# A decoder layer on one core: the first stage runs its pairs of sequences further ahead of the attentions

## The chip, the core and the metric

The kernel runs on one core of a Trainium2 chip. The metric is the device time of one execution in microseconds (us), lower is better. The core's engines work side by side and meet only through semaphores: TensorE (PE, matmuls and transposes), VectorE (DVE), ScalarE (ACT), GpSimd (POOL) and SyncE (SP, which only starts DMAs here).

## The reference, cut to what matters

The input is 16 sequences of 128 tokens with 128 features. There are three stages, each with a residual and a layer norm behind it. The first ("mixer") and the second (attentions and feed-forward) look like this; the third, a small per-position network, isn't touched by the change.

```python
# first stage, per sequence
x = u @ W_in + b_in                       # 128 -> 3*128
uc = dw_causal_conv(x.T, short_w, short_b)   # 3 taps per channel
q, k, v = uc[:, :D], uc[:, D:2*D], uc[:, 2*D:]
v = dw_causal_conv(k * v, inner_w, inner_b)  # 4 taps
y = (q * v).T @ W_out + b_out
x1 = layernorm(u + y)
# second stage: 16 heads of 64, self attention, then cross attention
a = attention(x1, x1, mask, sa_wq, sa_wk, sa_wv, sa_wo, sa_bo)
x = layernorm(x1 + a, ln1_g, ln1_b)
a = attention(x, ctx, mask, ca_wq, ...); x = layernorm(x + a, ...)
x = layernorm(x + fc2(gelu(fc1(x))), ...)
```

## The kernel before, in words

There is no scheduler. Each engine has a list of steps written out by hand in `mixer_and_attentions`, the same loop over a period number `p` on every engine, and each engine works through its own list in order. A step's semaphore waits hold up whatever is behind it on that engine.

**Items.** There are 32 attention items: item n is the self attention of sequence n for n < 16, then the cross attention of n - 16. Period `p` has, on PE: `x_transpose(p-4)`, the two value products `v_half(p)`, four `unit`s (query and key products of the next pair of items, alternating in banks 0 and 1), the four transposes of the probabilities of item p-1, `out_proj(p-2)`, `scores(p+1)` and `p_v(p-1)`. DVE takes row maxima (`maxima`, four groups of four heads, the first two at the end of the period before), reciprocals, copies keys (`k_out`) and transposed probabilities (`pt_out`) out of PSUM, and does `residual(p-2)` with its statistics. ACT does the exponentials (`exps`, four groups), and copies queries, values and outputs (`q_out`, `v_out`, `ot_out`). POOL multiplies the probabilities by the reciprocals (`normalise(p, g)`) and does the power for the standard deviation, gains and shifts.

**The first stage** handles pairs m = 0..7 of sequences inside the same loop, one step of a pair every second period. `pair_of(p, lead)` gives pair m in period p = 2m - lead, and nothing otherwise. With the leads before (PROJECT 6, CONVOLVE 4, TRANSPOSE 3), pair m goes like this:
- p = 2m-6 (even): projections of channels 0 and 1 on PE (`projection`), `projected` on ACT, two earlier taps for each on DVE (`earlier_taps`);
- p = 2m-5 (odd): the same for channel 2, then on POOL `keys_values` (edge fix and the product k*v) and `output_bias`;
- p = 2m-4 (even): `inner_convolution` (DVE, four taps), `gate` (POOL), `mixer_output` (PE), `mixer_residual` and `mixer_statistics` (DVE), `mixer_deviation` (POOL), `mixer_shift` (DVE), `mixer_normal` (ACT, at the end of its list);
- p = 2m-3 (odd): `x1_transposes` (PE), `x1_high` (ACT) and `x1_low` (DVE), which split the result in two parts for the attention's products, and `mixer_residuals` (POOL).
The attention's products of pair m start in period 2m-2 and wait for `x1_low(m)` (semaphore x1lo).

**Period 0 is not the first.** The loop starts at FIRST = -7; units start in period -2. The tail of odd periods also splits raw input and weights into a high part (ACT: `x_high`, `weight_high`) and a low part (DVE: `x_low`, `weight_low`). Banks: 4 and 5 hold projections and the p_v products, 6 the values, 7 (W_BANK) everything 128 wide, and before the change `mixer_output` too; `x1_transposes` went to bank 5.

## Time and profile before

| what | value |
|---|---|
| median of 3 runs | 558.27 us (556.9 to 560.64) |
| the profiled execution's own time | 560.64 us |
| its span in the trace | 558.8 us |
| PE busy | 475.0 us, 85% of the span |
| DVE busy | 412.6 us, 74% |
| ACT busy | 370.5 us, 66% |
| POOL busy | 262.8 us, 47% |

The span is the time from the first to the last instruction; the metric adds 1.84 us around it. A period is best measured between the starts of two `scores` groups on PE: scores(0) starts at 42.75 us, scores(1) at 56.40, scores(2) at 70.10, scores(12) at 235.52. From there to the last one at 460.92 us a period takes 11.92 us. The names of tiles in the trace have their bank and pair numbers left out: `late_bank` is any PSUM bank, `R`, `N`, `C`, `G`, `KV` and `yT` are tiles of the first stage, `at_...` tiles of the attention.

### The profile page before, as it was taken

Reading aid. Unit: us, or ns where it says so; the run is one execution under the profiler, and the core shown is the slowest. Engines: PE = TensorE matmul, PEld = TensorE weight load, DVE = VectorE, ACT = ScalarE, POOL = GpSimd, SP = SyncE. Lnnn points to the kernel's source line nnn. Section 1 sums busy time; section 2 is a strip of 40 time slices with the busy share of each in tenths; the row PEclk is TensorE's granted clock in tenths of the full one; section 3 lists DMA queues with packets and bytes.
Section 4 is the critical chain, followed back from the end, with each engine's and each line's share of the span. In section 5 each row is a group of like instructions: output and inputs, shape, how many; then the busy total and the mean of one; then the engine's idle time right before and its main releaser. Section 6 shows DMA issues by size and latency. Waiting matters only on the chain. (4 is left out here: it accounts for less than half of the span.)

```text
span 558.8 us, 13934 instructions
## 1 busy us (share of the span) xinstructions
PE 475.0 (85%) x4518; PEld 433.8 (78%) x4518; DVE 412.6 (74%) x1925; ACT 370.5 (66%) x1390; POOL 262.8 (47%) x348
## 2 busy tenths in 40 slices
PE   1477778888788887899999999999999999989573
PEld 1376667777677877899999999999999987779462
DVE  3666787887869777787777887777887776468774
ACT  3335776938667484788888688887688886534534
POOL 0423364544645455454554445554545545333561
PEclk9988899999979998999999999999999999997765
DMA  7910000000000000060000000000000000050003
GB/s 220 272 64 2 1 2 2 2 1 2 0 2 2 2 1 2 2 110 4 3 2 2 1 4 1 2 1 2 3 2 2 1 4 0 1 156 2 3 18 75
DMA packets 14663, 13.64 MB, mean 24 GB/s; under 512 B 2816, under 2 KB 12288, under 8 KB 14464
## 3 DMA queue, kind: packets, MB, share of 16 engines
q1 hardware_dynamic: 14448, 12.49, 8.3%
q8 instruction: 37, 0.61, 0.5%
q14 instruction: 34, 0.28, 0.2%
q10 hardware_dynamic: 144, 0.26, 0.2%
HBM read 11.57 MB, written 1.18 MB: 23 GB/s over the span
## 5 line engine op out<-in xcount | busy, mean ns | idle before, releaser
L580 ACT ACTIVATE P<-P,at_negmax 128x128 f32<-128x128 f32 x512 | 198.9, 396 | 55.6 <-DVE at_negmax L723 55.6
L952 POOL TENSOR_TENSOR P<-P,at_inv 128x512 f32<-128x512 f32 x128 | 131.9, 1042 | 151.4 <-DVE at_inv L733 151.4
L749 DVE COPY at_PT<-late_bank 128x512 f32<-128x512 f32 x128 | 87.7, 687 | 33.3 <-PE late_bank L442 33.1
L723 DVE CUSTOM_DVE_ANT_0 P<-late_bank,maskb 128x128 f32<-128x128 f32 x512 | 111.6, 286 | 0.5 <-PE late_bank L459 0.5
L580 ACT ACTIVATION_READ_ACCUMULATOR P<-P,at_negmax 128x1 f32 x512 | 100.0, 195 | 0.0
L442 PE MATMUL late_bank<-ident,P 128*128 128x128 f32 x512 | 78.9, 279 | 15.2 <-DVE at_negmax L723 13.3
L442 PEld LDWEIGHTS late_bank<-ident,P 128*128 128x128 f32 x512 | 60.9, 143 | 23.1 <-issue 18.9
L459 PE MATMUL late_bank<-at_k,at_q 64*128 64x128 f32 x1024 | 65.8, 278 | 1.0 <-DVE at_k L741 1.0
L459 PEld LDWEIGHTS late_bank<-at_k,at_q 64*128 64x128 f32 x1024 | 59.7, 188 | 5.3 <-issue 1.8
L474 PE MATMUL late_bank<-at_PT,V 128*64 128x128 f32 x1024 | 63.0, 276 | 0.0
L474 PEld LDWEIGHTS late_bank<-at_PT,V 128*64 128x64 f32 x1024 | 55.2, 137 | 3.9
L590 ACT ACTIVATE at_q<-late_bank 128x512 f32<-128x512 f32 x64 | 37.8, 591 | 27.5 <-PE late_bank L75 27.5
L741 DVE COPY at_k<-late_bank 128x512 f32<-128x512 f32 x64 | 44.1, 689 | 13.4 <-PE late_bank L75 12.6
L723 DVE DVE_READ_ACCUMULATOR2_ANT at_negmax<- 128x1 f32 x512 | 42.5, 83 | 0.0
L970 POOL TENSOR_TENSOR at_N<-at_N,row_ln_g 128x128 f32<-128x128 f32 x32 | 15.2, 474 | 57.4 <-DVE at_N L774 57.4
L599 ACT ACTIVATE V<-late_bank 128x512 f32<-128x512 f32 x64 | 37.7, 589 | 0.0
L733 DVE RECIPROCAL at_inv<-at_total 128x4 f32<-128x4 f32 x128 | 21.2, 170 | 19.0 <-ACT P L580 18.9
L607 ACT ACTIVATE at_OT<-late_bank 128x512 f32<-128x512 f32 x64 | 34.2, 591 | 0.0
L490 PE MATMUL late_bank<-wo_sa,at_OT 128*128 128x128 f32 x256 | 31.2, 275 | 0.0
L490 PE MATMUL late_bank<-wo_ca,at_OT 128*128 128x128 f32 x256 | 31.2, 275 | 0.0
L648 ACT ACTIVATE N<-R,shift,rstd 128x128 f32<-128x128 f32 x16 | 7.0, 487 | 36.0 <-DVE shift L871 36.0
L1381 POOL TENSOR_TENSOR ffrstd<-ffmv,half_neg 128x4 f32<-128x4 f32 x16 | 16.3, 1019 | 30.9 <-DVE ffmv L1274 30.9
(179 smaller groups left out, 1109.2 us busy)
## 6 DMA issues: line engine op xcount, KB each, us to landing
ctxT_raw<-in_ctxT SPq DMA_DIRECT2D x1, 1024.0 KB, 8.9
out<-xres SPq DMA_DIRECT2D x4, 224.0 KB, 2.5
x<-in_xT SPq DMA_DIRECT2D x1, 768.0 KB, 7.5
xres<-in_x SPq DMA_DIRECT2D x1, 768.0 KB, 12.3
...
```

Source lines behind the costliest of these rows:

```text
L442: last = nc.tensor.transpose(banks[T_BANK[g % 2]][:, h * 128:(h + 1) * 128], P[:, n % 2, HQ * g + h, :], k.ident[:])
L459: last = nc.tensor.matmul(score_bank(h), q[rows, t % 2, h // 2, pair], kk[rows, t % 2, h // 2, pair], start=True, stop=True)
L474: last = nc.tensor.matmul(banks[O_BANK[h // 8]][part:part + 64, h // 2 % 4 * 128:(h // 2 % 4 + 1) * 128], V[:, n % 2, h * DH:(h + 1) * DH] ...
L490: last = nc.tensor.matmul(banks[W_BANK][:, 0:128], OT[:, n % 2, c, :], out_w[att(n)][:, c, :], start=(c == 0), stop=(c == H // 2 - 1))
L580: last = nc.scalar.activation(P[:, n % 2, h, :], P[:, n % 2, h, :], ACT.Exp, scale=-1.0, bias=negmax[:, n % 2, h:h + 1], accum_out=total[: ...
L590: nc.scalar.activation(q[:, t % 2, u:u + 2, :], banks[UNIT_BANK[0]][:].rearrange("p (h l) -> p h l", h=2), ACT.Copy, scale=NEG_SCALE).then ...
L599: nc.scalar.activation(V[:, n % 2, half * 512:(half + 1) * 512], banks[V_BANK][:], ACT.Copy).then_inc(v_ok, 1)
L607: nc.scalar.activation(OT[:, n % 2, 4 * o:4 * o + 4, :], banks[O_BANK[o]][:].rearrange("p (c l) -> p c l", c=4), ACT.Copy).then_inc(ot_ok, 1)
L723: last = nc.vector.tensor_tensor_reduce(P[:, n % 2, h, :], score_bank(h), k.maskb[:, cols(n)], scale=1.0, scalar=3.0e38, op0=ALU.add, op1= ...
L741: nc.vector.tensor_copy(kk[:, t % 2, u - 1:u + 1, :], banks[UNIT_BANK[1]][:].rearrange("p (h l) -> p h l", h=2)).then_inc(k_ok, 1)
L749: nc.vector.tensor_copy(PT[:, HQ * g:HQ * g + HQ, :], banks[T_BANK[g % 2]][:].rearrange("p (h l) -> p h l", h=HQ)).then_inc(pt_ok, 1)
L952: nc.gpsimd.tensor_tensor(tile, tile, inv[:, n % 2, HQ * g:HQ * g + HQ].unsqueeze(2).to_broadcast([128, HQ, 128]), ALU.mult).then_inc(norm ...
```

## The change

The leads of the first stage are now PROJECT 8, CONVOLVE 6, OUTPUT 5, TRANSPOSE 4 with FIRST = -9. A pair m goes: channels 0 and 1 at p = 2m-8 (even), channel 2 and k*v at 2m-7 (odd), convolution and gate at 2m-6 (even), output product, residual and statistics at 2m-5 (odd), normalisation, transposes and both splits at 2m-4 (even), `mixer_residuals` at 2m-3 (odd). `mixer_output` writes to bank 5 and `x1_transposes` to bank 7. Steps stand at other places in the lists.

```diff
-        FIRST, FIRST_UNITS = -7, -2
+        FIRST, FIRST_UNITS = -9, -2
-        PROJECT, CONVOLVE, TRANSPOSE = 6, 4, 3
+        PROJECT, CONVOLVE, OUTPUT, TRANSPOSE = 8, 6, 5, 4
-        C_BANK, X1T_BANK = (4, 5, 4), 5
+        C_BANK, OUT1_BANK, X1T_BANK = (4, 5, 4), 5, W_BANK
@@ p_v(n)
-                    wait(pe, x1lo, ...)
+                if pair_of(n + 1, OUTPUT) is not None:
+                    wait(pe, r1_ok, pair_of(n + 1, OUTPUT) + 1)
@@ out_proj(n)
-                if pair_of(n + 2, CONVOLVE) is not None:
-                    wait(pe, r1_ok, pair_of(n + 2, CONVOLVE) + 1)
+                if pair_of(n + 2, TRANSPOSE) is not None:
+                    wait(pe, x1lo, pair_of(n + 2, TRANSPOSE) + 1)
@@ PE's list
                 transposes(p - 1, 1)
-                if p >= 0:
-                    mixer_output(p, pair_of(p, CONVOLVE))
                 unit(p, 2)
+                x1_transposes(p, pair_of(p, TRANSPOSE))
                 transposes(p - 1, 2)
...
                 projection(p, pair_of(p, PROJECT), 1)
-                if p < 0:
-                    mixer_output(p, pair_of(p, CONVOLVE))
-                x1_transposes(p, pair_of(p, TRANSPOSE))
+                mixer_output(p, pair_of(p, OUTPUT))
                 out_proj(p - 2)
@@ ACT's list
                 q_out(p, 0)
-                exps(p, 2)
+                mixer_normal(pair_of(p, TRANSPOSE))
                 ot_out(p - 2, 0)
                 ot_out(p - 2, 1)
+                exps(p, 2)
+                x1_high(pair_of(p, TRANSPOSE))
                 q_out(p, 2)
                 v_out(p, 1)
                 projected(pair_of(p, PROJECT), 0)
                 projected(pair_of(p, PROJECT), 1)
                 projected(pair_of(p, PROJECT - 1), 2)
-                x1_high(pair_of(p, TRANSPOSE))
                 exps(p, 3)
-                mixer_normal(pair_of(p, CONVOLVE))
@@ DVE's list
                 pt_out(p - 1, 1)
-                reciprocals(p, 2)
-                mixer_residual(pair_of(p, CONVOLVE))
                 pt_out(p - 1, 2)
                 k_out(p, 3)
                 pt_out(p - 1, 3)
-                mixer_statistics(pair_of(p, CONVOLVE))
                 earlier_taps(pair_of(p, PROJECT), (0, 1))
                 earlier_taps(pair_of(p, PROJECT - 1), (2,))
                 x1_low(pair_of(p, TRANSPOSE))
+                mixer_residual(pair_of(p, OUTPUT))
+                mixer_statistics(pair_of(p, OUTPUT))
+                reciprocals(p, 2)
+                if p % 2 and p >= -5:
+                    x_low((p + PROJECT + 1) // 2)
+                if p in (-5, -4, -3):
+                    weight_low(SA[p + 5])
...
+                elif p in (2, 4, 6):
+                    weight_low(CA[p // 2 - 1])
+                elif p in (8, 10):
+                    context_low((p - 8) // 2)
                 residual(p - 2)
                 reciprocals(p, 3)
                 maxima(p + 1, 0)
                 maxima(p + 1, 1)
-                mixer_shift(pair_of(p, CONVOLVE))
+                mixer_shift(pair_of(p, OUTPUT))
-                if p % 2 and p >= -3:
-                    x_low((p + PROJECT + 1) // 2)
-                elif p in (1, 3, 5):
-                    weight_low(CA[p // 2])
@@ POOL's list
-                normalise(p, 0)
                 gate(pair_of(p, CONVOLVE))
-                for g in range(1, QUARTERS):
+                for g in range(QUARTERS):
                     normalise(p, g)
+                mixer_deviation(pair_of(p, OUTPUT))
                 inverse_deviation(p - 2)
-                mixer_deviation(pair_of(p, CONVOLVE))
-                mixer_residuals(pair_of(p, TRANSPOSE))
                 keys_values(pair_of(p, PROJECT - 1))
                 output_bias(pair_of(p, PROJECT - 1))
+                mixer_residuals(pair_of(p, TRANSPOSE - 1))
```

PE at the end of an even period, here p = 6, before; `w3` are the first stage's input weights, `wo_sa` the attention's output weights, L490 is `out_proj`, L459 is `scores`:

```order
L73 MATMUL late_bank5<-xT_hi,w3_hi 128x256 [waits mx_x1lo,mx_tap_ok,at_ot_ok]
L74 MATMUL late_bank5<-xT_lo,w3_hi 128x256
L75 MATMUL late_bank5<-xT_hi,w3_lo 128x256
L490 MATMUL late_bank7<-wo_sa,at_OT 128x128 [waits at_r_ok,mx_r1_ok,at_xT_lo,at_ot_ok]
L490 MATMUL late_bank7<-wo_sa,at_OT 128x128 x7
```

And in the changed kernel, where L491 is `out_proj`:

```order
L73 MATMUL late_bank5<-xT_hi,w3_hi 128x256 [waits mx_r1_ok,mx_tap_ok,at_ot_ok]
L74 MATMUL late_bank5<-xT_lo,w3_hi 128x256
L75 MATMUL late_bank5<-xT_hi,w3_lo 128x256
L491 MATMUL late_bank7<-wo_sa,at_OT 128x128 [waits at_r_ok,mx_x1lo,at_xT_lo,at_ot_ok]
L491 MATMUL late_bank7<-wo_sa,at_OT 128x128 x7
```

Nothing stands between the last projection and `out_proj` in either; `out_proj`'s wait on r1_ok (DVE's `mixer_residual`) became a wait on x1lo (DVE's `x1_low`).

DVE behind the last copies of an even period, p = 4, in the changed kernel (L743 `pt_out`, L822 `earlier_taps`, L872 `x1_low`, L877 `weight_low`, L755 `residual`):

```order
L735 COPY at_k<-late_bank1 128x512 [waits at_s_mm,at_u_mm]
L743 COPY at_PT<-late_bank3 128x512 [waits at_pv_mm,at_t_mm]
L822 SCALAR_TENSOR_TENSOR C<-late_bank4,taps,C 128x2x127 [waits mx_c_ok]
L822 SCALAR_TENSOR_TENSOR C<-late_bank5,taps,C 128x2x127 [waits mx_c_ok]
L822 SCALAR_TENSOR_TENSOR C<-late_bank4,taps,C 128x2x126 [waits mx_tap_part]
L822 SCALAR_TENSOR_TENSOR C<-late_bank5,taps,C 128x2x126 [waits mx_tap_part]
L872 TENSOR_TENSOR x1T_lo<-late_bank7,x1T_hi 128x256 [waits mx_x1hi]
L727 RECIPROCAL at_inv<-at_total 128x4 [waits at_exp_ok]
L877 TENSOR_TENSOR ca_wk_lo<-ca_wk_raw,ca_wk_hi 128x1024 [waits mx_w_hi]
L755 TENSOR_TENSOR at_R<-late_bank7,xres 128x128 [waits mx_res1_ok,at_n_ok,at_o_mm]
```

`x1_low` now stands in the same period as the four taps of channels 0 and 1, and behind them; `weight_low` stands ahead of `residual`, where before it stood between two pairs of maxima groups.

ACT in the middle of an even period, p = 4, in the changed kernel (L588 `q_out`, L646 `mixer_normal`, L605 `ot_out`, L578 `exps`, L654 `x1_high`, L597 `v_out`, L636 `projected`):

```order
L588 ACTIVATE at_q<-late_bank0 128x512 [waits at_s_mm,at_u_mm]
L646 ACTIVATE N1<-R1,shift1,rstd1 128x128 [waits mx_res1_ok,mx_xT1_mm,mx_shift1_ok]
L646 ACTIVATE N1<-R1,shift1,rstd1 128x128
L605 ACTIVATE at_OT<-late_bank4 128x512 [waits at_o_mm,at_pv_mm]
L605 ACTIVATE at_OT<-late_bank5 128x512 [waits at_o_mm,at_pv_mm]
L578 ACTIVATE P,at_total<-P,at_negmax 128x128 [waits at_max_ok]
L578 ACTIVATE P,at_total<-P,at_negmax 128x128 x3
L654 ACTIVATE x1T_hi<-late_bank7 128x256 [waits mx_xT1_mm]
L597 ACTIVATE V<-late_bank6 128x512 [waits at_pv_mm,at_v_mm]
L636 ACTIVATE C<-late_bank4,conv_bias,taps 128x256 [waits mx_y_ok,mx_c_mm]
L636 ACTIVATE C<-late_bank5,conv_bias,taps 128x256 [waits mx_y_ok,mx_c_mm]
```

`mixer_normal` moved from the end of the list, where it stood behind `exps(p, 3)` in the period of its statistics, to the period after them.

## Rows read from the trace of the kernel before

**Rows 1.** Windows: stretch and length, busy us by engine, PE clock, DMA, GB/s.

```profile
70.10:102.74 32.64, 26.56 (x267) 24.09 (x267) 25.89 (x113) 23.71 (x92) 15.55 (x19) 1.00 0.01 2
102.74:135.84 33.10, 26.71 (x271) 24.23 (x270) 26.68 (x117) 22.65 (x87) 17.68 (x23) 1.00 0.01 1
135.84:171.07 35.23, 29.30 (x270) 26.83 (x270) 26.42 (x117) 22.88 (x87) 17.65 (x23) 0.90 0.01 2
171.07:204.14 33.07, 26.68 (x271) 24.21 (x270) 26.68 (x117) 22.65 (x87) 17.65 (x23) 1.00 0.01 1
204.14:235.52 31.38, 26.96 (x262) 24.72 (x261) 24.31 (x110) 20.86 (x83) 17.48 (x23) 0.95 0.01 2
119.69:135.84 16.15, 13.21 (x134) 11.87 (x133) 11.57 (x56) 11.12 (x45) 6.65 (x9) 1.00 0.01 2
135.84:152.79 16.95, 13.51 (x139) 12.37 (x138) 14.85 (x63) 11.54 (x44) 11.02 (x14) 1.00 0.01 1
259.32:271.23 11.91, 11.91 (x128) 11.18 (x128) 9.40 (x48) 9.32 (x39) 5.98 (x8) 1.00 0.01 1
```

**Rows 2.** Waits from 70.1 to 221.5 us: who for whom, us, times, longest.

```profile
PE late_bank L442 <- DVE at_negmax L723: 12.2, 9, 2.0
PE late_bank L523 <- POOL yT L998: 8.5, 5, 2.1
```

**Rows 3.** Timeline of PE in two periods: start, us, what, idle before.

```profile
126.34 0.63 PE L442 MATMUL late_bank<-ident,P 128*128 128x128 f32 x4 [1.04 <-DVE at_negmax L723]
...
129.15 0.50 PE L73 MATMUL late_bank<-sa_wv_hi,x1T_hi 128*128 128x512 f32 x1 [1.47 <-ACT V L599]
...
133.96 1.95 PE L490 MATMUL late_bank<-wo_sa,at_OT 128*128 128x128 f32 x16
...
143.17 0.63 PE L442 MATMUL late_bank<-ident,P 128*128 128x128 f32 x4 [1.72 <-DVE at_negmax L723]
...
147.36 0.71 PE L523 MATMUL late_bank<-w_out,yT 128*128 128x128 f32 x4 [1.73 <-POOL yT L998]
```

**Rows 4.** Timeline of DVE in the same two periods.

```profile
134.71 0.99 DVE L828 SCALAR_TENSOR_TENSOR C<-late_bank,taps,C 128x254 f32<-128x254 f32 x2
...
135.61 0.41 DVE L878 TENSOR_TENSOR x1T_lo<-late_bank,x1T_hi 128x256 fp32r<-128x256 f32 x1
...
139.58 1.75 DVE L883 TENSOR_TENSOR ca_wv_lo<-ca_wv_raw,ca_wv_hi 128x1024 fp32r<-128x1024 f32 x1
...
143.64 1.77 DVE L842 SCALAR_TENSOR_TENSOR G<-KV,inner,G 128x256 f32<-128x256 f32 x3
...
152.39 1.64 DVE L828 SCALAR_TENSOR_TENSOR C<-late_bank,taps,C 128x254 f32<-128x254 f32 x4
```

**Rows 5.** Timeline of ACT in the same two periods.

```profile
124.50 0.88 ACT L648 ACTIVATE N<-R,shift,rstd 128x128 f32<-128x128 f32 x2 [4.38 <-DVE shift L871]
125.29 0.39 ACT L580 ACTIVATE P<-P,at_negmax 128x128 f32<-128x128 f32 x1
...
132.93 0.58 ACT L638 ACTIVATE C<-late_bank,conv_bias,taps 128x256 f32<-128x256 f32 x1
...
138.26 0.40 ACT L580 ACTIVATE P<-P,at_negmax 128x128 f32<-128x128 f32 x1 [0.93 <-DVE at_negmax L723]
```

**Rows 6.** Windows of POOL alone: its last seven steps of an odd period.

```profile
137.14:142.90 5.76, 5.67 (x7) 1.00 0.02 4
```

**Rows 7.** Timeline of POOL: the edge fix of channel 2's pair, between those.

```profile
140.22 1.19 POOL L987 TENSOR_TENSOR C<-C,edge 128x12 f32<-128x12 f32 x1
```

**Rows 8.** Timeline of the start: PE's first unit, DVE's first key copy, a wait.

```profile
26.69 0.58 PE L73 MATMUL late_bank<-x1T_hi,sa_wq_hi 128*128 128x256 f32 x1 [1.13 <-DVE x1T_lo L878]
...
30.86 0.68 DVE L741 COPY at_k<-late_bank 128x512 f32<-128x512 f32 x1
...
38.49 0.40 PE L73 MATMUL late_bank<-x1T_hi,sa_wq_hi 128*128 128x256 f32 x1 [2.91 <-ACT at_q L590]
```

**Rows 9.** Windows of the same start: clock of PE behind that wait.

```profile
38.49:42.75 4.26, 3.80 (x17) 3.44 (x18) 1.13 (x3) 1.58 (x4) 1.02 (x2) 0.60 0.00 0
```

More of the change, by code:

```diff
@@ L393, in _, with projected_by @@
             sp.wait_ge(ld_wo, 32)
-        def c_done(p):
-            return 3 * before((p + PROJECT) // 2) + (2 if p % 2 == 0 and (p + PROJECT) // 2 < NPAIR else 0)
+        def projected_by(p):
+            return 3 * before((p + PROJECT) // 2) + (2 if 0 <= (p + PROJECT) // 2 < NPAIR and p % 2 == 0 else
+                                                     3 if 0 <= (p + PROJECT) // 2 < NPAIR else 0)
         @block.tensor
@@ L519, in mixer_output @@
                 pe.wait_ge(y_ok, m + 1)
-                wait(pe, xT_lo, p - 3)
-                wait(pe, r_ok, p - 2)
+                wait(pe, ot_ok, 2 * (p - 1))
+                wait(pe, tap_ok, 3 * before(m + 2) - (1 if m + 2 <= NPAIR else 0))
                 for b in range(PAIR):
-                    last = nc.tensor.matmul(banks[W_BANK][:, b * 128:(b + 1) * 128], yT[:, b, :], w_out[:],
+                    last = nc.tensor.matmul(banks[OUT1_BANK][:, b * 128:(b + 1) * 128], yT[:, b, :], w_out[:],
                                             start=True, stop=True)
@@ L530, in x1_transposes @@
                 pe.wait_ge(n1_ok, m + 1)
-                wait(pe, ot_ok, 2 * (p - 1))
-                wait(pe, tap_ok, 3 * before(m + 2) - (1 if m + 2 <= NPAIR else 0))
+                wait(pe, xT_lo, p - 3)
+                wait(pe, r_ok, p - 2)
                 for b in range(PAIR):
```

36 lines of the change are left out of this document (11 added, 25 removed).

## The prediction, written before the changed kernel ran

> **What bounds the kernel now.** I read the windows first, cut at the starts of scores groups. Behind the first stage a period takes 11.91 us and PE is busy for all of it; while the first stage runs, a pair of periods takes 31.4 to 35.2 us and PE is busy for 26.6 to 29.3 of it [rows 1]. So that stretch, 70.10 to 235.52 us, is bound by waits between engines, not by one engine: DVE, the next busiest, has 26.7 of 33.1 us [rows 1]. PE's timeline says where a pair loses time [rows 3]. In the odd period: 1.04 us for the maxima, 1.47 for the copy of V. In the even period: 1.72 for the maxima, 1.73 for the gate's yT. The sums of the waits show that this repeats: 12.2 us for maxima in 9 waits, 8.5 for yT in 5 [rows 2].
>
> Each has its cause in the lists. ACT sat 4.38 us in front of mixer_normal, waiting for the shift of the same period, and only then began the next item's exponentials, at 125.29 [rows 5]; V's copy stands behind those. The maxima of the even period are split by a 1.75 us weight_low (or context_low) [rows 4]. The gate waits for a convolution that begins in the same period, 1.77 us of it in three taps [rows 4].
>
> **What goes.** All four. The convolution's product is used one period later, mixer_normal waits for a shift of the period before, and weight_low now runs between x1_low and residual, under PE's out_proj (1.95 us [rows 3]), where DVE would wait for o_mm anyway: 1.75 us against about 2, so I cost it at nothing in its new place. If out_proj no longer covers it, it costs its 1.75 again, in three periods (and twice more for context_low).
>
> **What comes.** out_proj of even periods waits for x1_low, which waits for ACT and then stands behind four taps. PE stands still there with scores and p_v queued behind it, and the next maxima, so everybody, wait. I follow one even period from the start of the out_proj before it (S):
> - to the first exponential: 4.3 us before (133.96 to 138.26 [rows 3, 5]). DVE now has mixer_residual, statistics and x_low ahead of its residual, about 2.9 us with the taps, where it had 1.3 (taps 0.99, x1_low 0.41 [rows 4]); out_proj covers half of the 1.6 more. I take 4.3 + 0.8 = 5.1.
> - ACT's list down to the last projected: 8.2 us before, from 125.29 to 133.51 [rows 5]; plus mixer_normal 0.88 less overlap, 0.8 [rows 5], plus x1_high 0.3 and a second projected 0.5: 9.8.
> - three of the four taps come behind that copy, 1.64 x 3/4 = 1.25, then x1_low 0.41 [rows 4], 0.2 for the hops: 1.9.
> - N1 is one buffer, and mixer_normal must wait until POOL has done both mixer_residuals of the pair before. These are now last on POOL's odd list: the seven steps from the last normalise to the bias take 5.76 us [rows 6], and the first stage's power, 0.7, joins them. POOL ends at S + 4.4 + 6.5 = S + 10.9, or a microsecond sooner if the edge fix doesn't take its 1.19 us [rows 7]. ACT arrives at about S + 9.5. I take 0.6 us between 0 and 1.5.
> Sum: 5.1 + 9.8 + 1.9 + 0.6 = 17.4, say **17.5 us for an even period** with taps, between 15.5 (DVE's delay and N1 both hidden) and 19. PE alone would be ready for out_proj after some 13 us, so it stands 3 to 4 us in one piece, longer than any wait in the trace of before.
>
> **An odd period** has nothing of this: out_proj follows mixer_output, whose yT is a period old. PE needs 11.91 [rows 1] + one projection 0.43 + the output product 0.47 = 12.8; **12.9**. It can't be less, and 14.5 is the upper bound, one of the old waits (1.47 [rows 3]) being back.
>
> **The weights' other user.** On edge fix rows: POOL's 128x12 operation took 1.19 us at 140.22, inside DVE's weight_low of 1.75 us from 139.58 [rows 7, 4]. The page SBUF — State Buffer of the Trainium skill, section Who interferes with whom, says that a DVE instruction with two SBUF inputs and a GpSimd instruction that reads SBUF exclude each other for their whole length, so the fix would take its unhindered time in the new order, weight_low being elsewhere; by that rule the N1 term would be 0.3 rather than 0.6, a microsecond in all, and the row agrees with it.
>
> **Start.** The loop has two more periods, and their work is not free: DVE does a third pair's taps and convolution and a second pair's statistics before the first key copy. By hand through DVE's list, with the durations of the same steps, PE's first unit moves from 26.69 to about 31 us, the first key copy from 30.86 to 38 [rows 8]. But the old start then lost 2.91 us in one wait of PE for ACT's q copy, stuck behind mixer_normal [rows 8]; that wait goes. scores(0) comes at 44.8 rather than 42.75, +2. Periods 0 and 1 (13.7 us each) have no out_proj and so not the new wait; they take 10.7 and 12.0 by the same steps, since mixer_normal and the gate don't hold them up: -4.6. Half clock once more: +1.1. scores(2) then starts at 68.6 instead of 70.10: **-1.5**, between +4 (the whole delay of DVE, 7, less the 2.9) and -4.
>
> **The pairs of periods**, each against its row [rows 1]:
> - 2+3, 4+5, 6+7: 3 x (17.5 + 12.9) = 91.2 against 32.64 + 33.10 + 35.23 = 100.97: -9.8.
> - 8+9: no projections and no taps, so x1_low comes after the last copy: 15.3 + 12.5 = 27.8 against 33.07: -5.3. The last pair's convolution is in period 8, not 10.
> - 10+11: only the last x1_low: 13.2 + 12.0 = 25.2 against 31.38: -6.2.
> Sum with the start: -9.8 - 5.3 - 6.2 - 1.5 = **-22.8 us**. Half of it, 11.5, comes from the emptier end, not from the middle.
>
> **The clock.** Behind the 2.91 us wait PE's granted clock averaged 0.60 up to 42.75, which is half rate, 1.2 GHz, for most of it [rows 8, 9]. Between 70 and 221 us the clock fell twice, though no wait there was over 2.1 us; the pair 6+7, with 0.90, took 2.1 us more than 4+5 [rows 1]. The new waits of periods 2, 4 and 6 are 3 to 4 us each. I expect two falls more than I counted, at 2.1 each: +4.3. The page TensorE: Matmul & The Clock Gate, section Why this matters for your kernels, warns of idle gaps between bursts of matmuls. By that rule every one of the three waits would bring a fall, 6.4 instead of 4.3; the rows of before can't say, as no such wait is in that stretch.
>
> **Sum.** -22.8 + 4.3 = -18.5 us. The profiled execution took 560.64, its span 558.8; 560.64 - 18.5 = 542.1. It is the slowest of three runs, 0.4% above their median 558.27, so against the median the forecast is 558.27 - 18.5 = **540 us**. Everything behind period 12 (attention at 11.91 a period, feed-forward) shifts and keeps its length; the late loads wait for mixer_residuals of the last pair, now in the tail of period 11, as before, and are used from period 16 on, four periods of 11.91 us later.
>
> **Rivals.**
> 1. *The new wait is a trade.* Even periods at 19 and odd at 14.5 (both upper bounds) make 33.5 per pair, what a pair has now. Only the emptier end is left: +0 for the three pairs, -11.5 for the rest, +3 for the start, +4 for the clock: 554. For it: three lists must meet in x1_low. Against: it needs old waits back whose causes are gone. 0.15.
> 2. *The clock rule.* Each wait of 3 to 4 us drops the clock and the odd period, then bound by PE, runs its first 5 to 8 us at half rate: 3 to 4 us in each of the periods 3, 5, 7, also 9 and 1, some 17 us instead of 4.3: 553. The window 38.49 to 42.75 speaks for it [rows 9], the many waits of 1.7 to 2 us without a fall against. The clock page named above would give this; 0.1.
> 3. *Slower:* mixer_normal behind POOL. If mixer_residuals end at S + 14 or later rather than S + 10.9 (POOL held by DVE's convolution and by its own normalise), ACT's list stands for 4.5 us with ot_out and exps behind it, even periods take 21.5, five of them: +20, and the start's +4: 558.27 - 18.5 + 20 + 5 = 565. It decides from 4 us of lateness on. POOL is busy for 17.7 of 33.1 us a pair [rows 1], which speaks against. 0.06.
> 4. *Start eats it:* DVE is full until scores(0), +7 there, rest as forecast: 549. 0.09.
> 5. *No new wait.* x1_low early enough, both periods at 13: another -12: 528. ACT's list, 9.8 us from its first exponential, excludes most of it. 0.08.
> The forecast itself, within 6 us, has 0.52.
>
> That the change doesn't do what it says can be left out: the lists show each step moved.
>
> **Range and chances.** 528 to 554 takes in the bounds of the even and odd periods and rivals 1, 2, 4 and 5, and leaves out the slower case and the outer half of the others. A measurement can tell about 1% from no change here, 5.6 us, so "faster" is below 552.7: the forecast, 4, 5 and about half of 1 and 2 give 0.82. Within 1%: 0.11. Above 563.8: 0.07.
>
> **What would show it.** scores(0) near 45 us and scores(2) near 69; scores(12) near 213 to 217 instead of 235.5. In PE's waits out_proj (L491) behind DVE's x1_low at 3 to 4 us, three or four times; no waits of PE for yT or V over 0.5 us; ACT's wait before mixer_normal gone or named POOL. Odd periods near 13, even near 17.5. It is wrong if even periods are above 19, if the clock shows half rate in every odd period, or if PE waits for maxima again as DVE has more in front of them.

## The result, and the profile after

The changed kernel takes **542.87 us** (median of 4 runs, 542.41 to 545.54), the kernel before in the same comparison 557.83: a ratio of 0.973 with a 95% interval of 0.969 to 0.978. Forecast were 540 us and 528 to 554. The profiled execution took 543.13 us with a span of 541.2; the one before 560.64 and 558.8. The sums of the page (busy us and share of the span by engine) show that it is mostly waits that went: PE runs the same 4518 matmuls and is busy for 5.7 us less (475.0 before), no other engine changes by more than 1.9, so 11.9 of the 17.6 us are time in which PE stood still. Where PE's 5.7 us come from isn't broken down here.

```profile
span 541.2 us, 13929 instructions
...
PE 469.3 (87%) x4518; PEld 430.9 (80%) x4518; DVE 413.1 (76%) x1925; ACT 368.6 (68%) x1390; POOL 262.0 (48%) x348
```

The windows, cut at the starts of the scores groups of periods 2, 4, 6, 8, 10 and 12, answer to [rows 1]; the last two lines are period 4 and period 5 alone.

```profile
70.51:102.77 32.26, 27.60 (x268) 25.48 (x267) 26.27 (x114) 23.64 (x90) 15.41 (x19) 0.95 0.01 2
102.77:132.78 30.01, 26.35 (x270) 24.18 (x270) 26.45 (x117) 22.29 (x87) 17.56 (x23) 1.00 0.01 2
132.78:164.29 31.51, 27.83 (x270) 25.65 (x269) 26.45 (x117) 22.40 (x86) 17.56 (x23) 0.95 0.01 2
164.29:191.94 27.65, 25.48 (x262) 23.09 (x261) 24.44 (x115) 20.82 (x83) 17.42 (x23) 1.00 0.01 1
191.94:217.57 25.63, 24.26 (x258) 22.61 (x257) 20.56 (x101) 19.74 (x82) 15.53 (x20) 1.00 0.01 2
...
102.77:120.07 17.30, 13.64 (x136) 12.19 (x135) 15.93 (x66) 11.76 (x45) 12.64 (x16) 1.00 0.01 1
120.07:132.78 12.71, 12.71 (x135) 11.99 (x135) 10.52 (x51) 10.53 (x42) 4.92 (x7) 1.00 0.01 3
```

An odd period is now full of PE (12.71 of 12.71 us). An even one has PE busy for 13.64 of 17.30 us and DVE for 15.93. DVE was the fullest engine of an even period before too (14.85 of 16.95 [rows 1], PE 13.51); now it is busy for 92% of it. The sums of the waits from 70.51 to 205.66 us (who for whom, us, times, longest) answer to [rows 2]: yT and V are gone, the waits for maxima fell from 12.2 to 3.4 us, and most of the gap has one name. (The tables call the four transposes of the probabilities L443 here, L442 in the kernel before.)

```profile
PE late_bank L491 <- DVE x1T_lo L872: 10.6, 5, 2.7
PE late_bank L443 <- DVE at_negmax L717: 3.4, 4, 1.8
```

Three timelines of period 4 (start, us, what, idle before) answer to [rows 3 to 7]: the end of the period on PE and DVE, then the middle on ACT.

```profile
109.01 0.63 PE L443 MATMUL late_bank<-ident,P 128*128 128x128 f32 x4 [0.63 <-DVE at_negmax L717]
...
118.12 2.02 PE L491 MATMUL late_bank<-wo_sa,at_OT 128*128 128x128 f32 x16 [2.56 <-DVE x1T_lo L872]
```

```profile
115.41 0.68 DVE L743 COPY at_PT<-late_bank 128x512 f32<-128x512 f32 x1
...
116.00 1.64 DVE L822 SCALAR_TENSOR_TENSOR C<-late_bank,taps,C 128x254 f32<-128x254 f32 x4
...
117.56 0.41 DVE L872 TENSOR_TENSOR x1T_lo<-late_bank,x1T_hi 128x256 fp32r<-128x256 f32 x1
...
117.97 1.19 DVE L877 TENSOR_TENSOR ca_wk_lo<-ca_wk_raw,ca_wk_hi 128x1024 fp32r<-128x1024 f32 x1
...
120.18 0.29 DVE L755 TENSOR_TENSOR at_R<-late_bank,xres 128x128 f32<-128x128 f32 x1 [1.01 <-PE late_bank L491]
```

```profile
110.67 0.88 ACT L646 ACTIVATE N<-R,shift,rstd 128x128 f32<-128x128 f32 x2 [0.36 <-POOL x L1013]
...
113.95 0.37 ACT L654 ACTIVATE x1T_hi<-late_bank 128x256 fp32r<-128x256 f32 x1
```

ACT has x1_high done at 114.32. DVE runs without a gap from the last copy of P over the four taps to x1_low; PE has nothing to do from 115.56 on. Behind x1_low DVE does weight_low and then still waits 1.01 us for out_proj: weight_low is free there.

What this makes of the forecast, counted at the starts of scores groups: scores(0) 46.91 instead of 42.75 (+4.2), scores(2) 70.51 instead of 70.10 (+0.4), then the five pairs -0.4, -3.1, -3.7, -5.4, -5.8: scores(12) at 217.57 instead of 235.52, **-17.95**. The rest of the kernel takes 323.6 us, before 323.3. The start of scores(12) is the better measure of a kernel here, since the part behind it varies by itself by up to 3.6 us (last section); the table at the end of the experiments has it for every kernel.

### The profile page after: what moved, and what is told of

Same layout as the page of the kernel before. It is cut to its first block and busy times, and to the rows that moved or that the text cites. A ratio compares the mean times of both kernels' runs of the same rounds, so it can differ in the third digit from the quotient of the medians.

```text
span 541.2 us, 13929 instructions
## 1 busy us (share of the span) xinstructions
PE 469.3 (87%) x4518; PEld 430.9 (80%) x4518; DVE 413.1 (76%) x1925; ACT 368.6 (68%) x1390; POOL 262.0 (48%) x348
## 2 busy tenths in 40 slices
DMA packets 14663, 13.64 MB, mean 25 GB/s; under 512 B 2816, under 2 KB 12288, under 8 KB 14464
## 5 line engine op out<-in xcount | busy, mean ns | idle before, releaser
L578 ACT ACTIVATE P<-P,at_negmax 128x128 f32<-128x128 f32 x512 | 199.0, 397 | 93.5 <-DVE at_negmax L717 93.5
L942 POOL TENSOR_TENSOR P<-P,at_inv 128x512 f32<-128x512 f32 x128 | 136.4, 1076 | 129.1 <-DVE at_inv L727 129.0
L743 DVE COPY at_PT<-late_bank 128x512 f32<-128x512 f32 x128 | 87.2, 687 | 31.4 <-PE late_bank L443 31.4
L578 ACT ACTIVATION_READ_ACCUMULATOR P<-P,at_negmax 128x1 f32 x512 | 100.4, 196 | 0.0
L443 PE MATMUL late_bank<-ident,P 128*128 128x128 f32 x512 | 77.1, 274 | 6.2 <-DVE at_negmax L717 3.9
L443 PEld LDWEIGHTS late_bank<-ident,P 128*128 128x128 f32 x512 | 59.7, 141 | 13.7 <-issue 9.4
L491 PE MATMUL late_bank<-wo_sa,at_OT 128*128 128x128 f32 x256 | 34.6, 293 | 10.6 <-DVE x1T_lo L872 10.6
L491 PEld LDWEIGHTS late_bank<-wo_sa,at_OT 128*128 128x128 f32 x256 | 32.8, 208 | 11.6 <-issue 11.6
L588 ACT ACTIVATE at_q<-late_bank 128x512 f32<-128x512 f32 x64 | 37.6, 587 | 3.1 <-PE late_bank L75 3.1
L597 ACT ACTIVATE V<-late_bank 128x512 f32<-128x512 f32 x64 | 37.5, 586 | 0.0
L605 ACT ACTIVATE at_OT<-late_bank 128x512 f32<-128x512 f32 x64 | 34.1, 587 | 0.0
L755 DVE TENSOR_TENSOR at_R<-late_bank,xres 128x128 f32<-128x128 f32 x32 | 9.3, 290 | 30.4 <-PE late_bank L491 30.4
L491 PE MATMUL late_bank<-wo_ca,at_OT 128*128 128x128 f32 x256 | 31.2, 275 | 0.0
## 6 DMA issues: line engine op xcount, KB each, us to landing
xres<-in_x SPq DMA_DIRECT2D x1, 768.0 KB, 12.2
```

What stands on the lines that cost most here:

```text
L443: last = nc.tensor.transpose(banks[T_BANK[g % 2]][:, h * 128:(h + 1) * 128], P[:, n % 2, HQ * g + h, :], k.ident[:])
L491: last = nc.tensor.matmul(banks[W_BANK][:, 0:128], OT[:, n % 2, c, :], out_w[att(n)][:, c, :], start=(c == 0), stop=(c == H // 2 - 1))
L578: last = nc.scalar.activation(P[:, n % 2, h, :], P[:, n % 2, h, :], ACT.Exp, scale=-1.0, bias=negmax[:, n % 2, h:h + 1], accum_out=total[: ...
L588: nc.scalar.activation(q[:, t % 2, u:u + 2, :], banks[UNIT_BANK[0]][:].rearrange("p (h l) -> p h l", h=2), ACT.Copy, scale=NEG_SCALE).then ...
L597: nc.scalar.activation(V[:, n % 2, half * 512:(half + 1) * 512], banks[V_BANK][:], ACT.Copy).then_inc(v_ok, 1)
L605: nc.scalar.activation(OT[:, n % 2, 4 * o:4 * o + 4, :], banks[O_BANK[o]][:].rearrange("p (c l) -> p c l", c=4), ACT.Copy).then_inc(ot_ok, 1)
```

## The experiments

Four questions: what does each moved step bring by itself; what sets x1_low; what does the long wait do to the clock; and what bounds the version that comes out. All ratios are to the kernel before on the same chip.

### The parts, put into the kernel before

**b_low**: only the splits' new place. **b_normal**: only the place of mixer_normal, from the end of ACT's list to behind q_out of the next period. **b_both**: the two together.

```
# b_low, DVE's list
                 x1_low(pair_of(p, TRANSPOSE))
+                if p > 0 and p % 2:
+                    x_low((p + PROJECT + 1) // 2)
+                if p in (1, 3, 5):
+                    weight_low(CA[p // 2])
+                elif p in (7, 9):
+                    context_low((p - 7) // 2)
                 residual(p - 2)
...
-                elif p in (1, 3, 5):
-                    weight_low(CA[p // 2])
# b_normal, ACT's list
                 q_out(p, 0)
+                mixer_normal(pair_of(p, TRANSPOSE))
                 exps(p, 2)
...
-                mixer_normal(pair_of(p, CONVOLVE))
```

> The kernel before, with the low parts of input and weights (x_low, weight_low, context_low) of odd periods ahead of residual in DVE's list, nothing else. Theory 1 (waits of a pair add up, and this one is DVE's place alone): the 1.7 us wait for maxima in the even periods 2, 4, 6, 8 goes and 0.8 us of period 10's, 6 to 8 us in all, time 550 to 552. Theory 2 (the pair is bound by a loop through ACT and POOL, so that a wait taken away shows up at the next one, yT): under 2 us, 556 to 558.

Measured: 564.26 us, ratio 1.010 [1.004, 1.016]; about 6 us slower. DVE's timeline shows the splits in their new place:

```profile
136.61 0.43 DVE L794 TENSOR_TENSOR xT_lo<-x,xT_hi 128x256 fp32r<-128x256 f32 x1 [0.39 <-ACT xT_hi L629]
...
137.56 1.23 DVE L883 TENSOR_TENSOR ca_wv_lo<-ca_wv_raw,ca_wv_hi 128x1024 fp32r<-128x1024 f32 x1 [0.52 <-ACT ca_wv_hi L660]
...
138.70 0.28 DVE L761 TENSOR_TENSOR at_R<-late_bank,xres 128x128 f32<-128x128 f32 x1
```

out_proj started at 134.15 here and was done at 136.1, so the residual could have run 2.6 us earlier. PE's wait for the maxima falls to 0.79 us in the even periods, as expected, but its wait for yT rises from 1.72 to 2.43, and the clock falls four times between 140 and 223 us instead of twice. So neither expectation came true: the wait that was taken away came back larger at the next one. The slot under out_proj is not there in the old order: before, DVE reaches the residual just as the sum is ready, and two of the splits wait for ACT besides.

> The kernel before, with mixer_normal in ACT's list behind q_out(p, 0) of the next (odd) period instead of at the end of the even one, nothing else. Theory 1: ACT's 4.4 us in front of it go, the exponentials of the odd item start about 2 us sooner, and PE's wait for V (1.47 us) in periods 3, 5, 7, 9, 11 goes: 6 to 8 us, time 550 to 552. Theory 2: mixer_normal now stands in front of ot_out, x1_transposes and the split come later in the odd period, and p_v, which waits for x1_low, takes the time back: under 2 us, 556 to 558.

Measured: 544.53 us, ratio 0.975 [0.971, 0.979]. One step moved gives 13.7 us, nearly as much as the whole change (15.0) and twice what was expected. By scores(12), at 221.49 us, it is 14.0 of the 17.95 us, near four fifths; the profiled execution got the rest from a feed-forward that took 3.6 us less than in the changed kernel (last section). Its waits from 70 to 222 us:

```profile
PE late_bank L442 <- DVE at_negmax L723: 12.2, 9, 2.0
PE late_bank L523 <- POOL yT L998: 8.5, 5, 2.1
```

These two sums are what they were [rows 2]. What went is the copy of V, and ACT's 4.38 us [rows 5]: odd periods take 14.45 instead of 16.15, and the start is better by 2.6 us (scores(0) at 40.17, as the 2.91 us wait of [rows 8] is gone). The even periods keep their 16.9. Of the 14.0 us, 8.5 are the odd periods, 2.6 the start and 0.8 periods 0 and 1; 2.1 are a fall of the clock that isn't there in period 7.

> Both edits together on the kernel before, with its old leads. Theory L (the lists did it): 12 to 15 us, time 543 to 546, as good as the change, whose new leads bring only what the longer start costs. Theory P (the periods did it): these two bring at most 8 us, 549 or more, and the rest of the 15 us is the yT wait (1.7 us in five periods) and the emptier periods 8 to 11, which only the leads give.

Measured: 554.48 us, ratio 0.993 [0.990, 0.996]: the splits cost 10 us here, against 6 alone. Odd periods 14.2 to 14.5, but even ones 19.2 to 19.35 up to period 8. PE waits for yT for 1.83 us in period 2 and for 2.42 in each of 4, 6, 8 and 10; the clock falls behind these waits in periods 2 to 8, and not in 10. The time is in Theory P's range, but not for want of new periods: the splits' place takes back most of the 13.7 us that the other step gives alone.

### Parts taken back from the changed kernel

**a_nback**: mixer_normal back at the end of ACT's loop body, behind the shift of the same period, and mixer_residuals after it. **a_wback**: the splits back between the maxima and the taps. **a_res0**: the first pair's mixer_residuals one period earlier, so that ACT doesn't wait for them in the start.

```
# a_nback
-                mixer_normal(pair_of(p, TRANSPOSE))
                 ot_out(p - 2, 0)
...
                     feed_forward_high()
+                mixer_normal(pair_of(p, OUTPUT))
# and on POOL
-                mixer_residuals(pair_of(p, TRANSPOSE - 1))
+                mixer_residuals(pair_of(p, TRANSPOSE))
# a_wback
-                elif p in (2, 4, 6):
-                    weight_low(CA[p // 2 - 1])
...
                 mixer_shift(pair_of(p, OUTPUT))
+                if p in (2, 4, 6):
+                    weight_low(CA[p // 2 - 1])
# a_res0
-                mixer_residuals(pair_of(p, TRANSPOSE - 1))
+                mixer_residuals(pair_of(p, TRANSPOSE if p == -4 else TRANSPOSE - 1) if p != -3 else None)
```

> The changed kernel, leads as they are, with mixer_normal back at the end of ACT's list in the period of its statistics, so that ACT waits for the shift there, and mixer_residuals one period earlier with it. Theory L (one place in ACT's list was worth nearly all of the change: alone on the old kernel it gave 13.7 us): the change without it is worth little, 553 to 557. Theory P (new leads and lists bring their own share, the exponentials starting 2 us late cost about 1 us in each even period since DVE sets x1_low there): 547 to 550.

Measured: 546.07 us, 0.977 [0.974, 0.981], 3 us more than the changed kernel and below both expectations; the intervals of the two ratios overlap, but scores(12) comes 5.2 us later, at 222.78. ACT has its wait for the shift back, nearly whole:

```profile
140.94 0.88 ACT L646 ACTIVATE N<-R,shift,rstd 128x128 f32<-128x128 f32 x2 [3.90 <-DVE shift L865]
```

and PE's waits from 70 to 205 us show V back in each even period, with x1_low where it was:

```profile
PE late_bank L491 <- DVE x1T_lo L872: 9.1, 4, 2.6
PE late_bank L73 <- ACT V L597: 5.9, 5, 1.5
```

An even period takes 18.2 instead of 17.3. So the same wait of ACT, 3.9 us, costs 0.7 to 1.4 a pair here where the clock holds, 5.2 us at scores(12), where in the kernel before its removal was worth 14.0 there: DVE's list, not ACT's, leads to x1_low, and PE stands there in either case.

> The changed kernel, with weight_low and context_low back between the two halves of the maxima (behind mixer_shift, at the end of DVE's list), in the same periods. I had costed them at nothing in their new place under out_proj. Theory 1 (that place is free because DVE waits for out_proj there): here they put the maxima's second half 1.2 us later in periods 3, 5, 7, 9 and 11, where PE has nearly no slack, 0.8 to 1.2 us each: 546.5 to 549. Theory 2 (they are worth nothing in either place): 542.5 to 543.5.

Measured: 542.88 us, 0.972 [0.968, 0.975], no different from the change in its total. In each odd period it costs 0.5 to 0.6 (13.24 instead of 12.71), 2.7 us in the five of them. Two things hide that: period 6 has no fall of the clock here, although PE waits for x1_low as long as before, which gives 1.5 back, and the feed-forward gives 1.3 (last section). scores(12) is 1.3 us later. So the new place is worth half a microsecond a pair, near 2.7 us in all, half of what the first theory expected, and not nothing.

> The changed kernel, with mixer_residuals of the first pair alone one period earlier in POOL's list (period -4 instead of -3), ahead of the second pair's power and product. ACT waited 5.0 us for it in front of mixer_normal of the second pair, and PE 4.8 us for that. Theory 1 (this single buffer N1 set the start): scores(0) comes 2 us earlier, at 44.5 to 45 as I had forecast without it, and the time is 540.5 to 541.5. Theory 2 (DVE's list, full up to its first key copy at 37.5 us, sets the start anyway): scores(0) within 0.5 us of 46.9 and no change.

Measured: 541.74 us, 0.969 [0.965, 0.973]; scores(0) at 46.40 instead of 46.91, the rest alike. The changed kernel's start has this wait on ACT:

```profile
36.87 0.88 ACT L646 ACTIVATE N<-R,shift,rstd 128x128 f32<-128x128 f32 x2 [4.98 <-POOL x L1013]
...
37.80 0.69 PE L535 MATMUL late_bank<-ident,N 128*128 128x128 f32 x2 [4.83 <-ACT N L646]
```

Without it ACT and PE are earlier, but PE then stands before DVE's first key copy, which comes at 37.52 us here and at 37.47 in the changed kernel:

```profile
38.26 0.58 PE L73 MATMUL late_bank<-x1T_hi,sa_wk_hi 128*128 128x256 f32 x1 [2.08 <-DVE at_k L735]
```

5 us of waiting by two engines, and 0.5 us of them count: up to that copy, DVE's list sets the start.

### What sets x1_low

**a_x1_taps**: x1_low ahead of the taps. **a_x1_early**: ahead of the last copies too. In both ACT's list and every other step stay.

```
# a_x1_early (a_x1_taps: between the last pt_out and earlier_taps)
                 pt_out(p - 1, 2)
+                x1_low(pair_of(p, TRANSPOSE))
                 k_out(p, 3)
                 pt_out(p - 1, 3)
                 earlier_taps(pair_of(p, PROJECT), (0, 1))
                 earlier_taps(pair_of(p, PROJECT - 1), (2,))
-                x1_low(pair_of(p, TRANSPOSE))
```

> The changed kernel, with x1_low ahead of earlier_taps in DVE's list instead of behind it. Theory D (out_proj's new wait, 2.56 to 2.72 us in periods 2, 4, 6, is DVE's list: x1_high is done 2 us before DVE comes to x1_low): the wait shrinks by the four taps, 1.6 us, to about 1.0, three times, and with waits of 1 us the clock's two falls behind them (1.5 us each) are gone: 5 to 8 us, time 535 to 538. Theory A (ACT's list sets it, as my sum had it, three taps behind ACT's last copy): x1_low itself needs no projected copy, so it moves as well, but p_v then waits for the taps instead: under 3 us, 540 to 542.

Measured: 534.25 us, 0.956 [0.952, 0.960]. The wait of PE falls to 1.00 us in periods 2, 4 and 6, and the even period with it, to 15.76 us:

```profile
PE late_bank L491 <- DVE x1T_lo L872: 5.8, 5, 1.4
```
```profile
99.96:115.72 15.76, 13.64 (x136) 12.18 (x135) 15.28 (x66) 12.08 (x45) 11.10 (x16) 1.00 0.01 2
```

17.30 - 15.76 is 1.54, the 1.64 us of the four taps less what they overlap. At scores(12) the kernel is 7.4 us ahead of the changed one: about 4.8 from the three shorter waits and 3.0 from two falls of the clock that are gone, less 0.4 in the start. ACT's last projected copies begin 12.40 us behind scores(4) in both kernels (112.36 here, 115.17 there), so what moved x1_low is its place in DVE's list. It runs at 113.21, right behind DVE's last copy, though x1_high was done at 111.51. The clock doesn't fall once behind 68 us.

> The changed kernel, with x1_low still further ahead in DVE's list: between the third and the fourth copy of transposed probabilities. x1_high is done by then, so out_proj's wait (1.0 us left in periods 2, 4, 6 with x1_low ahead of the taps, 1.4 in 8 and 10) goes altogether. Theory W (each wait of PE taken away is time): 5.8 us less than with x1_low ahead of the taps, 528 to 529. Theory D (DVE now has taps, weight_low and residual in one piece behind its copies, 25.9 us of work per pair against PE's 25.8): in the even periods with taps nothing more is won, the odd period's transposes wait for maxima instead; only periods 8 and 10 give their 1.4 each: 531 to 532.

Measured: 530.82 us, 0.951 [0.948, 0.953]. PE's waits from 70 to 205 us:

```profile
PE late_bank L443 <- DVE at_negmax L717: 5.5, 7, 1.8
...
PE late_bank L491 <- DVE x1T_lo L872: 0.4, 2, 0.2
```

The wait for x1_low is gone with ACT's list as it was, so the copies of DVE were what x1_low still stood behind. Even periods take 14.5. But odd ones rise from 12.71 to 13.75: PE waits 0.7 us for the maxima of the odd period, as PE is on time at out_proj and weight_low behind x1_low no longer fits under it. Of 2.8 us gained in the even period 1 comes back in the odd one. c_late, below, takes those splits out of the stretch, and the odd periods are at 12.7 again.

### The clock

**a_fill** puts 16 transposes that nobody reads into a free bank ahead of out_proj's wait, in attention 0, 2 and 4. They fill all but 0.7 us of the idle time and change nothing else that PE waits for.

```
+                if n in (0, 2, 4):
+                    wait(pe, pt_ok, 4 * (n + 1) + 3)
+                    for _ in range(16):
+                        nc.tensor.transpose(banks[T_BANK[0]][:, 0:128], k.ident[:], k.ident[:])
                 if pair_of(n + 2, TRANSPOSE) is not None:
                     wait(pe, x1lo, pair_of(n + 2, TRANSPOSE) + 1)
```

> The changed kernel, with 16 transposes of the identity into a PSUM bank that nobody reads then, ahead of out_proj in periods 2, 4 and 6, in the 2.6 us in which PE waited for x1_low; they compute nothing that is used. 16 take 1.9 us at full clock, less than the wait. Theory C (the two falls of the clock, which made out_proj take 3.45 us instead of 1.95 in periods 2 and 6, came from PE standing idle in front of it): no fall there, 3 us less, 539.5 to 540.5. Theory N (they came from something else, or the falls only move): within 1 us of 543, or slower by the transposes if they are in the way.

First what the changed kernel shows of its clock: out_proj and the granted clock in period 2 and in period 4, behind waits of 2.72 and 2.56 us.

```profile
86.66:90.12 3.46, 3.46 (x16) 3.34 (x16) 1.05 (x1) 0.00 (x0) 1.93 (x1) 0.54 0.00 0
118.12:120.07 1.95, 1.95 (x16) 1.83 (x16) 1.05 (x1) 0.00 (x0) 1.93 (x1) 1.00 0.00 0
```

And period 6, behind 2.56 us again:

```profile
148.13 3.52 PE L491 MATMUL late_bank<-wo_sa,at_OT 128*128 128x128 f32 x16 [2.56 <-DVE x1T_lo L872]
```

The same 16 matmuls take 3.5 us at half clock (1.2 GHz) and 1.95 at 2.4 GHz; periods 2 and 6 are 2.3 and 1.5 us longer than period 4. With the transposes (median 539.57 us, 0.967 [0.962, 0.971]) period 6 takes as long as period 4, and no fall follows an out_proj. Period 6 of that kernel:

```profile
134.38:151.63 17.25, 15.42 (x152) 13.92 (x152) 15.92 (x66) 11.86 (x45) 12.58 (x16) 1.00 0.00 1
```

Its length stays 17.25 us, as DVE sets it: filled or not, PE arrives when x1_low does. In period 2 of the filled kernel the clock falls all the same, at 80 to 83 us, behind a wait of 1.84 us for the maxima, and again at 63 to 69 us; this execution thus has no gain over the changed kernel's (543.07 against 543.13 us) though its median is 3.3 lower, with intervals of the two ratios that still overlap. Nor does the missing fall of period 6 prove the filling right, as it is also missing in two kernels that fill nothing. Period 6 of a_wback, and of a_nback:

```profile
149.34 2.02 PE L491 MATMUL late_bank<-wo_sa,at_OT 128*128 128x128 f32 x16 [2.57 <-DVE x1T_lo L872]
```
```profile
152.78 2.02 PE L491 MATMUL late_bank<-wo_sa,at_OT 128*128 128x128 f32 x16 [2.56 <-DVE x1T_lo L872]
```

The changed kernel, a_res0, a_wback and a_nback have these waits unfilled. In period 2 (2.56 to 2.75 us) the clock falls behind all four; in periods 4 and 6 (2.56 and 2.57 us) behind two of eight. The best sign for idle time as the cause is period 2: in a_nback a fall at 79 us, behind a wait of 1.85 us for the maxima, is followed by a second one at 89 behind the open wait, in the filled kernel the one at 80 is followed by none. That idle time in front of out_proj brings the falls is thus likely and not shown, and what decides between equal waits stays open. The Trainium skill warns, in TensorE: Matmul & The Clock Gate, section Why this matters for your kernels, of idle gaps between bursts of matmuls; the falls here stand behind such gaps, but gaps of the same length stand there without one.

### How far either order goes

**b_ngate**: b_normal, and the gate ahead of the first normalise in POOL's list. **b_nglate**: that, and the cross-attention's weights split in periods 8 to 13, where the first stage runs out. **c_late**: the changed kernel with x1_low early, the first residuals early, and the same late splits.

```
# b_ngate, POOL's list, on b_normal
-                normalise(p, 0)
                 gate(pair_of(p, CONVOLVE))
-                for g in range(1, QUARTERS):
+                for g in range(QUARTERS):
                     normalise(p, g)
# b_nglate and c_late (ACT's and DVE's lists; context_* in 11, 12 and 12, 13)
-                elif p in (1, 3, 5):
-                    weight_high(CA[p // 2])
+                elif p in (8, 9, 10):
+                    weight_high(CA[p - 8])
...
+                if p in (9, 10, 11):
+                    weight_low(CA[p - 9])
```

> The kernel before with mixer_normal moved as in b_normal, and the gate ahead of normalise(p, 0) in POOL's list, as the changed kernel has it, leads as before. Theory 1: yT comes 1.0 us sooner (one normalise) in periods 2, 4, 6, 8 and 10, PE's wait for it falls from 1.7 to 0.7: 5 us less than b_normal's 544.5, 539 to 540.5. Theory 2: PE waits for the next thing (normalise(p, 0) itself isn't wanted until the next period, but the third transposes are near) and under 2 us are won: 542.5 to 544.

Measured: 536.32 us, 0.960 [0.956, 0.964]. PE's waits from 70 to 222 us:

```profile
PE late_bank L442 <- DVE at_negmax L723: 12.2, 9, 2.0
PE late_bank L523 <- POOL yT L998: 3.0, 4, 1.0
```

Even periods take 15.85 instead of 16.93. The long yT wait was for POOL's list order, a normalise of about a microsecond ahead of the gate, and needed no period more between the steps. It is 3 us more than expected: at scores(12) the kernel is 9.6 us ahead of b_normal, and two falls of the clock (at 60 and 203 us) are gone with it, with waits of up to 2.00 us for the maxima still there.

> The old leads with lists at their best as far as known: b_ngate, and the cross attention's weights and context split in periods 8 to 13 instead of 1 to 9, ahead of residual. Theory L (leads aren't needed): the 1.7 us wait for maxima in even periods shrinks by weight_low's 1.2 us in periods 2, 4, 6, 8 and 10; 5 us less than b_ngate, 533 to 535, as good as the changed kernel with x1_low ahead (534.3). Theory P (with the convolution in the period of its use the gate's chain stays the bound): 537 or more, and only the new leads get below.

Measured: 531.48 us, 0.952 [0.949, 0.955]. Even periods 14.58; the maxima's long wait, 1.72 us, was the weight_low between its halves [rows 4]. PE's wait for yT rises with it from 0.64 to 1.05 us, as the next one in the chain.

> The changed kernel with x1_low between the copies (a_x1_early), the first pair's mixer_residuals one period earlier (a_res0), and the cross attention's weights and context split in periods 8 to 13, where DVE is busy for 9.4 us of 11.9. Theory D (DVE bounds the pairs of a_x1_early): 1.2 us less in each of periods 2, 4, 6, and context_low and 0.5 us of the start besides: 526 to 528. Theory W (it is chains of waits, not DVE's sum): within 1.5 us of a_x1_early, 529.5 to 531.

Measured: **528.06 us**, 0.945 [0.942, 0.948], the best of all: even periods 14.5, odd 12.7. PE's largest wait left in the middle:

```profile
PE late_bank L443 <- DVE at_negmax L717: 3.9, 5, 1.8
```

So the wider spacing as tuned here is worth 3.4 us over the narrow one as tuned here, 5.2 by scores(12): its pairs take 27.2 us against 29.1, its emptier end helps, and its start costs 5.5 us (scores(0) at 45.55 against 40.05). That the spacing itself is needed for this isn't shown: in b_nglate PE still waits 5.7 us for maxima and 5.1 for yT, and no run tried further orders of its lists.

All kernels in one table: the median, the starts of scores(0) and scores(12), the rest behind scores(12), and the falls of the granted clock between 70 and 222 us, all but the median from the profiled execution.

| kernel | median us | scores(0) | scores(12) | rest | falls |
|---|---|---|---|---|---|
| before | 557.83 | 42.75 | 235.52 | 323.3 | 2 |
| the change | 542.87 | 46.91 | 217.57 | 323.6 | 2 |
| b_low | 564.26 | 42.02 | 239.89 | 321.9 | 5 |
| b_normal | 544.53 | 40.17 | 221.49 | 320.0 | 1 |
| b_both | 554.48 | 40.70 | 230.97 | 320.0 | 4 |
| a_nback | 546.07 | 45.96 | 222.78 | 322.3 | 2 |
| a_wback | 542.88 | 46.83 | 218.87 | 322.3 | 1 |
| a_res0 | 541.74 | 46.40 | 217.09 | 323.6 | 2 |
| a_x1_taps | 534.25 | 46.65 | 210.16 | 322.3 | 0 |
| a_x1_early | 530.82 | 46.94 | 207.38 | 322.3 | 0 |
| a_fill | 539.57 | 46.94 | 217.61 | 323.6 | 1 |
| b_ngate | 536.32 | 40.21 | 211.91 | 323.3 | 0 |
| b_nglate | 531.48 | 40.05 | 207.55 | 321.9 | 0 |
| c_late | 528.06 | 45.55 | 202.39 | 323.7 | 0 |

## Why the prediction was right, and where it was off

- **The sum.** Forecast -18.5 us against the profiled execution, measured -17.5 there. The 540 missed the median by 2.9 us, 1.0 of it in the sum; the rest because the profiled execution of before lay 2.4 us above its median and that of after 0.3 above its own. That distance should have been a term.
- **Odd periods**: 12.9 forecast, 12.65 to 12.71 measured, full of PE. Right, with its reason.
- **Even periods**: 17.5 forecast, 17.3 where the clock holds. The size was right and **its step incomplete**: the sum leads through ACT's list to the last projected copy, and "three of the four taps come behind that copy". ACT's side came out as summed, the copies done at 116.20, 15.4 us behind the start of out_proj, where 15.5 were forecast. But DVE comes to the taps at 116.00 by its own list, having stood still for 0.15 us since 105.06, and is busy for 15.93 of 17.30 us. The two lists meet within 0.2 us, so that the sum through one of them gave the right size is luck. What a shorter wait needs is told by the runs: moving x1_low ahead of the taps gives 1.54 us a period (a_x1_taps), moving it between the copies takes the whole wait away (a_x1_early), both with ACT's list as it is. I followed ACT's list to the end and DVE's not. The wait of PE is 2.6 us and not 3 to 4, as PE itself is at out_proj after 14.7 us, not 13.
- **N1**: 0.6 forecast, 0.36 measured in period 4, at most 0.7 in the others (the 0.3 of the sentence on the edge fix is nearer). The fix takes 0.21 us in its new place instead of 1.19 [rows 7].
- **The start** was mis-sized: scores(0) +4.2 instead of +2. DVE's delay was right, the first key copy coming at 37.47 where 38 was forecast. The step that failed is the one behind it: 6.8 us from that copy to scores(0) in the forecast, 9.44 in the trace (11.89 before). The wait of 2.91 us is gone, but PE, standing until 37.80, runs at half clock to 42 us, and DVE waits for it for 2.29 and 1.07 us ahead of the second and the fourth key copy. Periods 0 and 1 gave 3.8 back, forecast 4.6. a_res0 shows that the one wait in the start that I had not seen is worth 0.5.
- **weight_low at nothing**: right in the changed kernel (residual still waits 1.01 us behind it). The reason given, that DVE would wait for o_mm anyway, holds only because PE is late there itself: in b_low the same place cost 6 us, and in a_x1_early, with PE on time, about 1 a pair. a_wback puts the old place at 0.5 a pair.
- **The other pairs**: 27.8 and 25.2 forecast, 27.65 and 25.63 measured. These two pairs brought 11.2 of the 17.95 us, 11.5 forecast; b_normal, with no emptier end, has 3.4 of them (its pairs take 31.38 and 29.67 us there against 33.07 and 31.38), so not all of it is the emptier end.
- **The clock**: two falls more, +4.3. Measured are two falls in the stretch, +2.3 and +1.5, as many as before, where [rows 1] has one of 2.1. The three pairs together took 93.8 us, where 91.2 + 4.3 were forecast. Rival 2, a fall in every period, would have needed the odd periods to begin at half clock, and both falls were over by the end of out_proj.
- **Rivals.** The trade (1): no old wait came back. Slower (3): POOL's residuals end at most 0.7 us late, not 4. Start eats it (4): scores(0) is 4.2 us late, not 7, and periods 0 and 1 gave 3.8 of it back. No new wait (5) is what a_x1_early makes of the kernel, 530.8; DVE's list and not ACT's, as I had written, excluded it.
- **What the forecast did not see**: that most of the gain hangs on one step. b_normal has 13.7 of the 15 us (14.0 of 17.95 at scores(12)) without any wider spacing; the spacing in the form given adds an emptier end and a shorter odd period, and pays in the start and in a new wait. What a forecast of the whole change can't tell, a forecast of each step by itself could have: ACT's 4.38 us were in [rows 5], and with mixer_normal behind q_out they go in either kernel.

## What to carry to other kernels

Before widening the distance of a pipeline, look for the one instruction that waits in an in-order list with others' work behind it, and move that alone: here it gave four fifths of the gain by scores(12), nine tenths by the medians. A step is free in a slot only as long as its engine is idle there for another's sake; when that other gets faster, or was never late, the step costs its whole length. When several lists meet in one step, follow each of them to it, the fullest engine first.

## What the runs showed of the chip

- **After the same wait PE runs at half clock or doesn't.** Waits of 2.72 and 2.56 us were followed by it and another of 2.56 wasn't; the filled kernel shows a fall behind 1.84 us, b_both one behind 1.83 and three behind 2.42, with a fourth 2.42 without. a_x1_taps, its longest wait there 1.4 us but for one of 1.85, shows none, and neither does b_ngate with one of 2.00 and three of 1.72.
- **The feed-forward takes its own clock.** From scores(12) on the kernels named here do the same work, yet that part took 320.0 us in b_normal and b_both, 322.3 in a_wback, 323.3 before and 323.6 after, each in one profiled execution. The difference is in the feed-forward, where the granted clock goes between half and whole. Windows of the same 10 us, 270 us behind scores(12), in the changed kernel and in b_normal:

```profile
487.57:497.57 10.00, 10.00 (x59) 0.75 0.01 2
```
```profile
491.49:501.49 10.00, 10.00 (x68) 0.83 0.01 2
```

  So kernels of which one is 3.9 us ahead at 220 us (the changed one against b_normal) can end within 0.3 us of each other in span. Differences of up to 3.6 us between two executions here are not proof of anything in the part that was edited; the starts of the scores groups are.
- **DVE and POOL slow each other.** A normalise of POOL takes 1.93 us beside weight_low, 1.04 earlier in the same period, and 1.04 in a_wback, where no weight_low runs beside it. The first product of DVE's convolution, read from SBUF beside POOL's mixer_residuals, takes 0.83 instead of the 0.40 of the kernel before:

```profile
105.22 1.04 POOL L942 TENSOR_TENSOR P<-P,at_inv 128x512 f32<-128x512 f32 x1 [0.20 <-DVE at_inv L727]
...
118.14 1.93 POOL L942 TENSOR_TENSOR P<-P,at_inv 128x512 f32<-128x512 f32 x1 [3.10 <-DVE at_inv L727]
```
```profile
109.13 0.83 DVE L832 TENSOR_SCALAR G<-KV,inner,inner_b 128x256 f32<-128x256 f32 x1
```

  The Trainium skill states that, in SBUF — State Buffer, section Who interferes with whom: an instruction of DVE with two SBUF inputs and one of POOL that reads SBUF exclude each other. The normalise of 1.93 us agrees with it; the convolution's product is a form with one input on DVE's side, which by the same page of the Trainium skill contends only in a faster mode.
